# Turning the tiles of a quantized MLP with DRAM round trips and VectorE block transposes instead of TensorE transposes

## The reference

```python
xn = layernorm(x)                       # no scale
# branch 1: state-space scan, then an MLP with exact gelu
a = xn + ssm_scan(rmsnorm(xn, scale1))  # 16 states per channel, plus D * u
a = a + gelu(rmsnorm(a, scale2) @ w1 + b1) @ w2 + b2     # 512 -> 2048 -> 512
# branch 2: gated MLP on FP4 values (blocks of 16 features share a scale; 8 magnitudes)
g = silu(q(xn) @ q(w_gate).T) * (q(xn) @ q(w_up).T)      # 512 -> 1408
f = q(g) @ q(w_down).T                                   # 1408 -> 512
out = x + a + f
```

## Time and profile before

| | us |
|---|---|
| device time, median of 3 runs (lowest, highest) | 3289.08 (3286.53, 3289.84) |
| device time of the profiled execution | 3286.65 |
| its span, first to last instruction | 3284.9 |
| PE busy | 3140.0 (96%) |
| DVE busy | 1962.9 (60%) |
| ACT busy | 1085.5 (33%) |
| POOL busy | 1074.8 (33%) |
| head: up to window 1 | 0 to 114 |
| windows 1 to 178 | 114 to 1845 |
| second half | 1845 to 3285 |

### The profile page before, as it was taken

One profiled execution on the slowest core, in us unless ns is written; L12 is line 12 of the kernel. 1 busy time (PEld: TensorE's weight loads), 2 busy tenths in 40 slices (PEclk: granted clock), 3 DMA queues, 4 the chain that ended last, 5 costly groups with the idle time before them and its releaser, 6 DMA issues.

```text
span 3284.9 us, 43359 instructions
## 1 busy us (share of the span) xinstructions
PE 3140.0 (96%) x15340; PEld 2530.9 (77%) x15340; DVE 1962.9 (60%) x4369; ACT 1085.5 (33%) x1908; POOL 1074.8 (33%) x1037
## 2 busy tenths in 40 slices
PE   5789899999998999999999999999999999999999
PEld 3577777778876777777777788888888888888887
DVE  7788788887775666666677654444444444444442
ACT  5335555544443333333332322112221212122211
POOL 7545455555453444444444311101111110111100
PEclk9999999999999999999999999999999999999999
DMA  4121222226654455455543422222222222222210
GB/s 118 42 62 59 89 89 62 88 70 163 164 157 102 132 148 145 130 151 137 130 117 78 125 52 42 52 38 50 52 48 49 48 47 52 42 52 42 52 20 26
DMA packets 594855, 272.65 MB, mean 83 GB/s; under 512 B 425040, under 2 KB 516432, under 8 KB 592080
## 3 DMA queue, kind: packets, MB, share of 16 engines
q1 hardware_dynamic: 594640, 269.88, 33.1%
HBM read 193.75 MB, written 76.05 MB: 82 GB/s over the span
## 4 chain that ended last, share of the span: by engine, by line
PE 61%; DVE 19%; POOL 7%; issue 6%; ACT 3%; DMA 1%; SPq 1%; DVEq 0%; ACTq 0%; POOLq 0%
PE bank L831 21%; PE bank L815 21%; PE bank L687 9%; PE bank L709 4%; POOL qa L1450 4%; DVE qs L937 3%; POOL qa L1456 3%; DVE qa L954 3%; DVE qa L909 2%; DVE qb L962 2%; DVE sg L901 2%; DVE qs L948 2%; PE bank L751 2%; PE bank L659 1%; DVE qs L942 1%
## 5 line engine op out<-in xcount | busy, mean ns | idle before, releaser
L815 PE MATMUL bank<-hT,Wp 128*128 128x512 f32 x3072 | 749.4, 393 | 1.4 <-ACT gf L1401 1.3
L831 PE MATMUL bank<-Wp,G 128*128 128x512 f32 x3072 | 743.5, 391 | 0.0
L831 PEld LDWEIGHTS bank<-Wp,G 128*128 128x128 f32 x3072 | 576.7, 188 | 125.6
L815 PEld LDWEIGHTS bank<-hT,Wp 128*128 128x128 f32 x3072 | 572.2, 188 | 122.8 <-ACT gf L1401 1.8
L687 PE MATMUL bank<-XT,Wg 128*128 128x512 f32 (+1 forms) x2148 | 532.4, 397 | 28.3 <-DVE XT L969 15.0
L1152 DVE CAST G<-gf 128x512 fp32r<-128x512 f32 x256 | 110.4, 431 | 749.5 <-PE bank L831 748.2
L709 PE MATMUL bank<-Wd,HT 128*128 128x512 f32 x2112 | 527.6, 399 | 12.3 <-POOL HT L1464 12.3
L687 PE MATMUL bank<-XT,Wu 128*128 128x512 f32 (+1 forms) x2148 | 516.6, 390 | 22.4 <-DVE sg L901 22.4
L687 PEld LDWEIGHTS bank<-XT,Wg 128*128 128x128 f32 x2148 | 400.3, 192 | 127.5 <-DVE XT L969 24.1
L687 PEld LDWEIGHTS bank<-XT,Wu 128*128 128x128 f32 x2148 | 403.1, 191 | 111.0 <-issue 29.9
L709 PEld LDWEIGHTS bank<-Wd,HT 128*128 128x128 f32 x2112 | 395.4, 191 | 106.2 <-POOL HT L1464 13.3
(11 more groups left out here) (111 smaller groups left out, 2838.3 us busy)
## 6 DMA issues: line engine op xcount, KB each, us to landing
px<-in_L_attn_x_dram SPq DMA_DIRECT2D x128, 256.0 KB, 2.9
xin<-in_L_attn_x_dram SPq DMA_DIRECT2D x128, 256.0 KB, 3.7
sT<-r_K SPq DMA_DIRECT2D x128, 256.0 KB, 4.2
r_Z<-xin SPq DMA_DIRECT2D x64, 256.0 KB, 2.2
r_U<-ub SPq DMA_DIRECT2D x16, 1024.0 KB, 6.6
sU<-r_U SPq DMA_DIRECT2D x32, 512.0 KB, 5.0
r_Y<-sY SPq DMA_DIRECT2D x16, 1024.0 KB, 5.7
xl<-in_L_attn_x_dram SPq DMA_DIRECT2D x64, 256.0 KB, 3.0
```

The costliest lines, as they stand in the source:

```text
L815: ins = e.matmul(bk[:], Wp[f][wh][:, 0, k * P:(k + 1) * P], hT[xh][b % 2][:, k, :], start=(k == 0 and p_ == 0), stop=(k == KD - 1 and p_ = ...
L831: ins = e.matmul(ACC[j][:], G2[gh][:, n % 2, j * P:(j + 1) * P], Wp[f][wh][:, 1, :], start=(f == 0 and p_ == 0), stop=(f == 15 and p_ == 2))
```

## The change

The 60 x tiles of the windows and tiles 4 to 63 of the second half are no longer turned by PE. Each tile, after dequant (`qa`) or after `tile_root` (`xl`), is stored to DRAM (`r_X`, `r_H`, two places each) by one DMA. SP waits for the store and issues four reads, one for each quarter q of 32 features in every 128: partitions 32q to 32q + 31 receive the 32 features 32q to 32q + 31 of each 128 as runs of 128 bytes. A DVE transpose of 128x512, which turns each 32x32 block within itself, then completes the turn.

In the windows the schedule of a tile that enters in window s becomes: store in SP's s + 1 (`tile_out`, waiting for dequant), read in SP's s + 2 (`tile_back`) into the tile's own `xin` slot, DVE `x_turn` in s + 3 into `XW`, an fp32 view of the memory of the low buffer `XT1`, ACT `x_high`, POOL `x_low` (subtraction in place). An `xin` slot is kept until `x_turn`, so the slots are given by `PLACE`, and the next load into a slot follows three windows after an x tile entered. Tiles enter at -9, -7, -3, -2 of each round instead of -7, -4, -2, -1. Weight tile 28 moves to the head (33 jobs); only w29 to w33 are still turned by PE in windows. `TAPS` avoids windows s with s - 3 in `SIDE` (was s - 2); SP's stores of the taps move to the start of its window, and the K row is stored one window earlier. Six instead of three small steps of the inverse roots are done per window up to window 13.

In the second half `h_turn` is used for tiles 0 to 3 only. For the others `quadrants` (SP, at part 1) stores and reads back, and `tile_low` begins with the DVE transpose into PSUM. The iterations of the three parts are (2, 3, 6), (4, 5, 8), (8, 9, 12), (10, 11, 14) for the four tiles of a batch.

```diff
-SIDE.update({NF * i + o: ("x", 4 * i + j) for i in range(2, NB) for o, j in ((-7, 0), (-4, 1), (-2, 2), (-1, 3))})
+SIDE = {1: ("w", 29), 2: ("w", 30), 3: ("w", 31), 4: ("w", 32), 5: ("x", 4), 6: ("w", 33), 7: ("x", 5), 8: ("x", 6),
+        10: ("x", 7)}
+SIDE.update({NF * i + o: ("x", 4 * i + j) for i in range(2, NB) for o, j in ((-9, 0), (-7, 1), (-3, 2), (-2, 3))})
+PLACE = [q % 2 if q < 6 else (q + 1) % 2 for q in range(len(SIDES))]
-TAPS = [s for s in range(K0, S0) if s - 2 not in SIDE][0:32]
+TAPS = [s for s in range(K0, S0) if s - 3 not in SIDE][0:32]
 def mlp_steps(n):
     b, f = n // 16, n % 16
+    at = [(2, 3, 6), (4, 5, 8), (8, 9, 12), (10, 11, 14)]
+    return [(4 * (b + 1) + j, part) for part in (2, 0, 1) for j in range(4) if at[j][part] == f]
...
+            def tile_out(m):
+                n = XPOS[m]
+                e.wait_ge(s_ph, m + 1)
+                e.dma_start(r_X[n % 2], qa[:, m % 4]).then_inc(d_so[n % 2], 16)
+
+            def tile_back(m):
+
+                n = XPOS[m]
+                e.wait_ge(d_so[n % 2], 16 * ((n + 1) // 2))
+                e.wait_ge(s_pa, m + 1)
+                for q in range(4):
+                    e.dma_start(xin[32 * q:32 * q + 32, place(m)].rearrange("p (k r i) -> p k r i", k=KD, r=4),
+                                bass.AP(r_X.tensor, n % 2 * P * D + 32 * q, [[D, 32], [P, KD], [32 * D, 4], [1, 32]])
+                                ).then_inc(d_xb[place(m)], 16)
...
+            def quadrants(t):
+
+
+                X = xl[slot(t)]
+                n = (t - 4) // 2 + 1
+                e.wait_ge(s_hs0, t + 1)
+                e.dma_start(r_H[t % 2], X[:]).then_inc(d_ho[t % 2], 16)
+                e.wait_ge(d_ho[t % 2], 16 * n)
+                for q in range(4):
+                    e.dma_start(X[32 * q:32 * q + 32].rearrange("p (k r i) -> p k r i", k=KD, r=4),
+                                bass.AP(r_H.tensor, t % 2 * P * D + 32 * q, [[D, 32], [P, KD], [32 * D, 4], [1, 32]])
+                                ).then_inc(d_hi[t % 2], 16)
...
             def window(s):
                 k = s - S0
+                if side(s - 2) in XPOS:
+                    tile_back(side(s - 2))
+                for i in range(16):
+                    if s == TAPS[2 * i + 1] + 2:
+                        kernel_w_out(i)
+                    if i % 4 == 3 and s == TAPS[2 * i + 1] + 2:
+                        kernel_row(i // 4)
...
+                if side(s - 1) in XPOS:
+                    tile_out(side(s - 1))
...
-                if side(s - 2) is not None:
+                if side(s - 2) in TPOS:
                     turn(side(s - 2))
...
-                for t, part in mlp_steps(n):
-                    if part == 2 and t < NT:
-                        h_turn(t)
...
+            def x_turn(m):
+
+                n = JOBS[m][1] // 2
+                e.wait_ge(d_xb[place(m)], 64 * returns(m))
+                if n >= 3:
+                    e.wait_ge(s_gu, last(n - 3) + 1)
+                e.transpose(whole(m), xin[:, place(m)].rearrange("p (k c) -> p k c", c=P)).then_inc(s_xt, 1)
...
-                if low_x is not None:
+                if low_x in TPOS:
                     low(low_x)
+                elif low_x is not None:
+                    x_turn(low_x)
...
+                if t >= 4:
+                    e.wait_ge(d_hi[t % 2], 64 * ((t - 4) // 2 + 1))
+                    if t < 6:
+                        e.wait_ge(s_z, NT)
+                    else:
+                        e.wait_ge(s_hlo, t - 1)
+                    e.transpose(T[:], xl[slot(t)][:]).then_inc(s_hs, 1)
                 e.wait_ge(s_hhi, t + 1)
...
+            def x_high(m):
+                e.wait_ge(s_xt, XPOS[m])
+                e.activation(job_dst(m)[0], whole(m), ACT.Copy).then_inc(s_xh, 1)
...
+            def x_low(m):
+                hi, lo = job_dst(m)
+                e.wait_ge(s_xh, XPOS[m])
+                e.tensor_tensor(lo, whole(m), hi.bitcast(F32), ALU.subtract).then_inc(s_xlo, 1)
...
                 dequant(h)
+                if side(s - 3) in XPOS:
+                    x_low(side(s - 3))
```

More of the change, by code:

```diff
@@ L78 @@
 NLOAD = [sum(k != "h" for k, _ in HEAD[:m]) for m in range(NJ)]
-TURNS = [m for m, (k, _) in enumerate(JOBS) if k != "h"]
+TURNS = [m for m, (k, _) in enumerate(JOBS) if k == "w" or m < NJ and k == "x"]
+XTURNS = [m for m, (k, _) in enumerate(JOBS) if k == "x" and m >= NJ]
+XPOS = {m: n + 1 for n, m in enumerate(XTURNS)}
 TPOS = {m: n + 1 for n, m in enumerate(TURNS)}
@@ L205, in build @@
             Wu.append([sbt(actx, f"Wu{f}{h}", [P, KD, P], F32R) for h in range(2)])
-        XT = [sbt(actx, f"XT{h}", [P, 3, KD, 2 * P], F32R) for h in range(2)]
+        XT = [sbt(actx, "XT0", [P, 3, KD, 2 * P], F32R)]
+        with ExitStack() as wctx:
+            XW = sbt(wctx, "XW", [P, 3, KD, 2 * P])
+        XT.append(sbt(actx, "XT1", [P, 3, KD, 2 * P], F32R))
         xin = sbt(actx, "xin", [P, 4, 512])
@@ L346, in turned, with place, loads, returns @@
         def turned(m):
[L347 to L351, removed]
-            return b[:, 0:job_width(m)]
+            return (bank[(5, 7)[TPOS[m] % 2]] if m < NJ else GB)[:, 0:job_width(m)]
+        def place(m):
+            return PLACE[SIDES.index(JOBS[m])]
+        def loads(m):
+            return PLACE[:SIDES.index(JOBS[m]) + 1].count(place(m))
+        def returns(m):
+            return sum(place(p) == place(m) for p in XTURNS[:XPOS[m]])
         def job_in(m):
@@ L357, in job_in @@
                 return qa[:, m % 4, 0:n]
-            return xin[:, m % 4 if m < NJ else SIDES.index(JOBS[m]) % 2, 0:n]
+            return xin[:, m % 4 if m < NJ else place(m), 0:n]
         def wait_qa(e, m):
@@ L541, in prepare @@
                     z_load(t + 1)
+                if part == 1 and t >= 4:
+                    quadrants(t)
                 if part == 2:
@@ L587, in window @@
                             e.dma_start(r_Y[v // 2], sY[:].rearrange("p t k -> p (t k)")).then_inc(d_sYo, 16)
-                if s in SIDE and SIDES.index(SIDE[s]) + 1 < len(SIDES):
-                    side_load(SIDES.index(SIDE[s]) + 1)
+                for q, p in enumerate(EARLIER):
+                    if p is not None and s == SWIN[SIDES[p]] + (3 if SIDES[p][0] == "x" else 0):
+                        side_load(q)
             load_w(0)
@@ L786, in h_turn @@
                 X = xl[slot(t)]
-                T = bank[7] if t < 4 else [bank[5], bank[6]][t % 2]
                 e.wait_ge(s_hs0, t + 1)
@@ L930, in biggest @@
                 elif JOBS[m][0] == "w":
-                    q = SIDES.index(JOBS[m])
-                    e.wait_ge(d_xs[q % 2], 16 * (q // 2 + 1))
+                    e.wait_ge(d_xs[place(m)], 16 * loads(m))
                 else:
@@ L1081, in window @@
                         todo.extend(batch_rsqrt(rooted(t) - 1))
-                for step in todo[0:3]:
+                for step in todo[0:6 if s < 14 else 3]:
                     step()
-                del todo[0:3]
+                del todo[0:6 if s < 14 else 3]
                 if PRE0 <= s < PRE0 + 12 and (s - PRE0) % 3 == 1:
@@ L1327, in window @@
                 k = s - S0
-                if side(s - 3) is not None:
+                if side(s - 3) in TPOS:
                     high(side(s - 3))
```

81 lines of the change are left out of this document (38 added, 43 removed).

## The result

The changed kernel takes 3250.8 us (median of four runs, 3248.06 to 3252.99) where the kernel before takes 3288.26: a ratio of 0.9884, 95% interval 0.9869 to 0.99. It is faster by 37.5 us; 54 were forecast, 3233 us, and the range 3203 to 3264 holds the time. The profiled execution has a span of 3250.7 us, 34.2 less than before.

| stretch | before, us | after, us | difference | forecast |
|---|---|---|---|---|
| head, windows 1 to 10 | 212.2 | 213.5 | +1.3 | 0 |
| windows 11 to 96 | 772.8 | 775.2 | +2.4 | 0 |
| of it, windows 27 and 28 | 29.8 | 17.0 | -12.8 | -8 |
| of it, windows 65 to 96 | 272.2 | 289.7 | +17.4 | +11 (late reads) |
| change of stage, 97 to 100 | 58.5 | 52.2 | -6.3 | -3 |

The account below looks back on a forecast made before the run. DVE's chain within a window was taken as the bound up to about window 97, PE after it. From 3286.65 us, -27 + 0 + 0 - 3 - 21 - 3 = -54 gave 3233 us, range 3203 to 3264.

Parts of the forecast that it names:

- B: Rival: the first half gives nothing, its stalls take back the gain; only the second half's 27 are left, 3260 us; 17%.
- D: Rival: the second half doesn't follow, PE idles there and all 27 us and a little more are lost; 3262 us; 4%.
- Second half: 60 turns leave PE at 0.48 or 0.41 us each, with DVE's transposes and the reads hidden: -27 us.
- Windows 11 to 96: Windows bound by DVE (11 to 97 in the prediction): four effects sum to 0, bounds -19 and +15 us.
- (c): Windows 11 to 97: reads of six tiles come late, their stores queued behind U's: +11 us, bounds 0 and 17.
- (b): Windows 11 to 97: POOL's subtraction pushes the scaling where tap sums share the window: +8 us, bounds 0 and 17.
- (d): Window 27: the K row, stored one window earlier and ahead of SP's other work, ends POOL's wait: -8 us.
- (a): Windows 11 to 97: DVE's waits for ACT's high half vanish: -11 us.
- Change of stage: Windows 97 to 100: DVE's longest tile wait goes, a late read takes most of its place: -3, bounds -8 and +3.
- State windows: Windows 101 to 162: the 27 us excess goes, 0.5 us comes through for each of 12 tiles: -21, bounds -27 and -8.
- A: Rival, late reads: reads in 128-byte runs land late and stall the first half; at 8.5 us landing 3329 us; 5%.
- C: Rival: all cover holds, POOL's subtraction and late reads cost nothing, state windows give 27: -81, 3206 us; 15%.

Follow-up runs that it names:

- second_start: The changed kernel with the last two stores of Z ahead of the loads of weights 12 to 15 and PE's last down product before its third mlp1: 3246.4 us.
- second_only: The kernel before with the second half of the change alone, the first half untouched: 3261.3 us.
- u_after_read: The changed kernel with each store of U except the last moved behind the tile reads, at the head of the next window: 3235.0 us.
- acts_low: The changed kernel with POOL's subtraction in the first half replaced by a plain ACT copy (wrong low halves): 3243.4 us.
- krow_late: The changed kernel with the row of K stored one window later, still at the head of SP's window: 3253.8 us.
- read_before_tw: The changed kernel, but tiles stored in odd state windows are read back in that window, between the loads of V and those of T and W: 3223.0 us.
- no_read: The changed kernel without the four reads of a tile in the first half, so wrong tiles are multiplied there: 3204.4 us.
- first_only: The changed kernel with the second half's turns back on PE, the first half of the change alone: 3276.8 us.
- krow_head: The kernel before with SP's stores of the taps at the head of its window, in the windows they had: 3278.8 us.
- combined: The changed kernel with U's stores behind the reads, reads between the loads of V and T, and the second half's start reordered: 3205.3 us.

## Why the prediction was right, and where it was wrong

The range held and the sign was right. But the main case's own bounds were 3215 to 3250, and 3250.8 lies just past them: the range held through the room that it left for rivals B and D, and 37.5 us is well short of 54. Step by step:

**Second half, -27.** Right in mechanism and size: alone it gave 27.2 us, and 25.1 of its span's 26.9 lie in its own stretch. Within the changed kernel 22.9 were left, with three stalls of 2.54, 2.11 and 0.47 us at its start (second_start gives 3.7 back). The prediction looked for trouble "at each batch's first block", from late reads, and there was none; the start itself it left out. The shorter last windows are only part of that: second_only, whose windows are those of before, has the three stalls too, at 1.29, 1.40 and 0.50 us, and the kernel before has one of 1.35. The cover itself held: no transpose waits (L1202, idle 0.0), and PE is busy all the time from 1900 us on.

**Head and windows 1 to 10, 0.** +1.3. The 3.5 us of a job became 2.7, and windows 1 to 10 gave 1.4 back where some 4 were taken.

**Windows 11 to 96, 0.** +2.4, and that this is near 0 is luck in part: two terms were off by 5 us in opposite directions. The four effects came out as follows. (c), late reads beside U: 15.8 us by u_after_read where 11 was forecast. The six tiles are the six that were named (entering at 68, 70, 74, 86, 90, 92), and in no tap window was a read late. (b), POOL's subtraction: 7.5 us by acts_low between windows 11 and 96 where 8 was forecast, although a third of it, 2.6, lies where no taps are and half of that within the traces' scatter. (d), the K row: 12.8 where 8 was forecast, and the reason given was wrong: not the earlier window but the head of the window, 10.5 us of it even without anything else. The prediction saw only the first row: the second had held POOL for 3.20 us in window 39 of the kernel before, and there krow_late prices the earlier window at 4.4 us. (a) has no run of its own. Its waits are as forecast: DVE has eight waits of over 0.3 us for ACT's high half in windows 11 to 96 of the kernel before, 10.5 us in all, and none after. What is left of +2.4 after the other three is 2.4 - 15.8 - 7.5 + 12.8 = -8.1, where -11 was forecast; that is a remainder, not a measurement, and the second row of K is in it. That the change as a whole doesn't pay where DVE is the bound is shown: with the late reads gone, windows 65 to 96 take 273.8 us and took 272.2 before.

**Change of stage, -3.** -6.3. Here 5.5 more were lost to a read that came 6.68 us late; that it takes the place of the old wait was foreseen.

**State windows, -21.** This is the step that failed, in its size. The mechanism was right on both sides. The excess of 27 us was indeed all due to the turning or the old load order: read_before_tw and no_read both take 629.5 us, 29.2 less than before. And the reads were late for the reason given, behind the loads of T and W. Wrong was: "I take 4 us of margin and let 0.5 us through for each of 12 tiles". The late reads cost 25.7 us, not 6. Three things were too small. DVE's stalls were not 2 to 5 us at 12 tiles but 0.79 to 7.04 at 14, the longest in part because the reads landed more slowly there than elsewhere (up to 7.13 us from the first issue to the last landing). The margin is not 4 us: PE waits 3.97 when DVE stalled 5.96, 4.24 for 7.04, 1.61 for 4.70, 3.27 for 5.25, 2.07 for 5.65, 1.37 for 5.01 and 0.45 for 2.57, while stalls up to 2.04 and one of 3.28 cost nothing, so it lies between 2.0 and 3.6 us. And some of what comes through is paid twice: PE's waits in this stretch sum to 17.0 us in seven pairs of windows, the excess of these pairs to 25.7. Of the other 8.7, 8.1 stand behind the four waits of 2.07 to 4.24 us, where the granted clock falls to 0.50 (1.2 GHz) in the wait or within 1.2 us behind it; behind the three waits of 0.45 to 1.61 us the clock is whole, and they cost 0.2 more each. The prediction had no such term, and its bounds for this step, -27 and -8, did not hold -3.5.

**Tail, -3.** -5.3.

**The rivals.** A, late reads: refuted, 2.6 us to landing in the median and 5.39 at most. The sentence on the Trainium skill ("DMA: Bandwidth & Descriptors", "Specifications"), that transfers want 512 bytes or more, spoke for A. Here runs of 128 bytes, four DMAs of 64 KB, land in 2.4 to 2.6 us where one 256 KB store in whole rows lands in 2.0 to 2.1; no run here shows what they cost other transfers, nor why four of them took up to 7.13 us in the state windows. B, the first half gives nothing: first_only gives it 11.7 us, but krow_head, which turns its tiles as before, has 6.7 of them (by the spans 9.2 of 11.1). The turning itself, as it was scheduled and with all else that came with it, brought 2 to 5 us, less than these medians can settle; so B was nearly right on the turning and wrong on the sum. C, all cover holds: refuted for the changed kernel, but its number, 3206, is what combined takes with the cover put in order (3205.3). That is luck in part: of C's 19 us in windows 11 to 96 combined has 12.8, and the change of stage, the state windows and the tail each give some 2 us more than C took. D: refuted by the blocks at 2.77 without a step. The rule of the Trainium skill ("VectorE: DVE Perf Modes", "Rules for kernel authors") to leave 128x128 transposes to TensorE would have left the 27 us of the second half, where PE is the bound, unused; between windows 65 and 96, where DVE is, the turns taken off PE gain nothing, and the rule costs nothing.

## What to carry to other kernels

Moving work off the bound engine by way of DRAM costs little in landing time where no large loads run beside it; it costs a place in a queue of DMAs, so write down what stands between the store and its reads before you count the gain. Put first what an engine waits for within a few microseconds, and behind it the large stores and the loads with windows to spare: here that order, with one block of PE's moved, was worth 45 us, more than the change. And a wait of TensorE can cost more than itself: beside the state work the four waits of 2.07 to 4.24 us cost 1.8 to 2.6 us each on top, in clock, and the three shorter ones 0.2.

## What the runs showed of the hardware

The DMA issued right behind a 1 MB store of U sat in issue for 4.03 to 4.92 us in the changed kernel, whichever it was (a tile's store, a load of x, a load of `a`), where the median of all issues is 0.56.

Four reads of 64 KB in runs of 128 bytes took a median of 4.56 us from the first issue to the last landing in the state windows of read_before_tw, and 5.08 to 7.13 us for nine of the eleven tiles of the changed kernel whose reads were issued close behind the loads of W (4.39 and 4.41 for the other two). What makes them slow wasn't tested.

After PE had been idle for 3.97 us, the next three groups of matmuls ran with a granted clock of 0.50 (1.2 GHz) for some 5 us, then at full speed again; 1.09 us became 1.98. After the wait of 2.54 us at 1842.20 the block took 4.49 us instead of 2.93. After one of 2.11 us, at 1869.53, the block took 2.99, so not every wait of two microseconds costs it: beside the state work one of 2.07 us did. Which do wasn't settled.

A DVE transpose of 128x512 in float32 takes 0.72 us into PSUM and 0.70 from SBUF to SBUF: the target makes no difference that counts.
